# The attention heads' output turned by DMA instead of TensorE: rows of features in memory, sums beside them, division and split on GpSimd and VectorE

## Chip, cores and metric

One core of one Trainium2 chip. The metric is the device time of one execution in microseconds (us), median of several runs.

## What is computed

`x` is 2 sequences of 1024 tokens with 512 features, all in float32. Six sublayers follow one another, each on the layer norm of `x` and each added to `x`:

```python
x = x + 0.5 * _L0_ffn_ref(_layernorm(x))    # one 512x512 product, columns scaled
x = x + _L0_attn_ref(_layernorm(x))         # 32 heads of 16, 8 key heads, rotary, causal, then @ w_o.T + b_o
x = x + 0.5 * _L0_ffn_ref(_layernorm(x))
x = x + 0.5 * _L1_ffn_ref(_layernorm(x))    # 512x512 product and 8 rank-16 experts, top 2
x = x + _L1_attn_ref(_layernorm(x))         # 8 heads of 32, causal, then @ w_o.T + b_o
x = x + 0.5 * _L1_ffn_ref(_layernorm(x))
```

The part that the change touches is the end of both attentions: `out = softmax(scores) @ v`, and `out @ w_o.T + b_o`.

## The kernel before

The five engines run their own programs, tied by semaphores. The two sequences (`b`) go one after the other; a sequence is three chains of 128-token tiles with an attention behind each of the first two: FFN_A and the products of QKV0, the first attention (`A0`), WO0, FFN_B, MOE_A and the products of QKV1, the second attention (`A1`), WO1 and MOE_B. Every product is three passes: an operand is split into a high part, rounded for TensorE's fast float32 form, and the low rest (hi x hi, hi x lo, lo x hi).

**An attention** works in units: 8 units of 4 heads in `A0`, 4 units of 2 heads in `A1`. A unit has two halves `c` of 512 queries; half 0 has 4 steps, half 1 has 8, one for each block of 128 keys (`steps`, 12 per unit). For a step TensorE makes the scores (L983, L977), ScalarE the exponentials into `probs` (L1431), GpSimd the causal mask of the diagonal blocks (L1542), and TensorE, two or three steps later, the value products into the PSUM bank `heads` (L999). There the heads stand as rows: the features of each head and beside them, through a column of ones in `v_mem`, the sum of its exponentials. When a half is done, ScalarE copies `heads` to `heads_raw` (L1418).

**The ring.** Softmax needs each row's maximum ahead of its exponentials. About one unit ahead TensorE makes the scores a second time for that, into three PSUM banks in turn (`ring`, L871), and VectorE reduces each bank (`maxes`, L1204 for masked ones, L1208 for the rest). Twice per unit VectorE makes the shifts (L1247 to L1253), TensorE turns them (L876), VectorE copies them out (`shiftT`, L1217), and SyncE stores them as operand rows of the scores. A third kind of item stands in the ring: `norm`, one per half of a unit. TensorE turns `heads_raw` with four transposes (L881), VectorE takes the reciprocals of the sums (L1227) and multiplies (L1232) into `features`, tokens in rows. `plan_ring` fixes the order of all items, and where among the steps they stand; item i is written only when item i-3 has been read (`ring_free`), and TensorE runs its list in order:

```python
kind, u, n = a.ring[i - 3]
read, m = {"max": (s["max_done"], u * a.unit_max_ops + a.max_ops_to[n]), "shift": (s["shiftT"], 2 * u + n + 1),
           "norm": (s["normed"], 2 * u + n + 1)}[kind]
pe.wait_ge(read.sem, read.at(b, m))
```

**The product of WO** (WO0, WO1): for each tile `turn_x` transposes `features` (L765, four transposes in WO0 and two in WO1), ScalarE copies the high part (L1315), VectorE subtracts the low part (L1055), TensorE makes 12 (WO0) or 6 (WO1) matmuls (L779 to L781), and VectorE adds the result to `x` (L1071), to which GpSimd has added the bias (L1484). `prod` has two banks, so tile t waits for the addition of tile t-2. In a chain the engines go by ticks: tick i holds the transposes of tile i, the product of tile i-1 and, on VectorE, the addition of tile i-2.

**SyncE** issues every DMA, in one order: in the first attention the rows of the shifts, and for unit u+3 the queries, once unit u's scores are done; the weights of FFN_B and MOE_A in units 3 and 4.

The names that the change and the prediction use: `plan_ring` (L191 on), `load_shifts` (L598), `rotated_attention` (L648), `standard_attention` (L687), `turn_x` (L751), `begin` (L768), `ring_item` (L856), `ring_read` (L1187), and `attention` of each engine.

## Time and profile before

| | |
|---|---|
| median of 3 runs | 1358.18 us (1355.22 to 1362.18) |
| the profiled execution | 1344.81 us, of which the span from the first to the last instruction 1343.1 us |
| TensorE busy (matmuls, weight loads) | 1205.7 us (90%), 753.2 us (56%) |
| VectorE busy | 953.5 us (71%) |
| ScalarE busy | 671.2 us (50%) |
| GpSimd busy | 375.2 us (28%) |
| mean granted TensorE clock | 0.928 |
| bytes moved by DMA | 76.20 MB |

Engines in the rows: PE is TensorE's matmuls, PEld its weight loads, DVE VectorE, ACT ScalarE, POOL GpSimd, SP SyncE. The matmuls overlap one another in the rows, so the distance from start to start tells what one costs. Time 0 is the first instruction. The first attention of the first sequence lies at 116 to 358 us, the second at 531 to 619 us.

### The profile page before, as it was taken

The page shows a single profiled execution, that of the slowest core. Times are in us where ns is not written, and L with a number is a line of the kernel's source. Part 1 is how long each engine was busy: PE and PEld are TensorE (multiplying, and loading weights), DVE is VectorE, ACT ScalarE, POOL GpSimd, SP SyncE. Part 2 cuts the span into 40 slices and gives each one's busy share as a digit, 9 for nine tenths or more (in the row PEclk, how much of TensorE's full clock was granted, in tenths as well). Part 3 has the DMA queues.
Part 4 walks back from the last instruction along what each step waited for, and adds up shares of the span by engine and source line. Part 5 has one row for each costly group of instructions (what it writes and reads, how often), then busy time and mean ns, then how long its engine had stood idle before and what let it go on. Part 6 is the DMA issues. An engine that isn't in the chain of part 4 may idle for free.

```text
span 1343.1 us, 21792 instructions
## 1 busy us (share of the span) xinstructions
PE 1205.7 (90%) x6800; PEld 753.2 (56%) x6800; DVE 953.5 (71%) x2990; ACT 671.2 (50%) x1023; POOL 375.2 (28%) x505
## 2 busy tenths in 40 slices
PE   4998999999899877998879999999988988879988
PEld 1875444443388865444868744444435887744368
DVE  5889889898166676653659798999962667576365
ACT  2621666666655452544436036666665554435542
POOL 0431411122254400114614323122213542002162
PEclk9996899999999997999979858999999999869999
DMA  8374411220010020100140742112200100120001
GB/s 317 120 196 87 125 29 26 57 65 3 1 49 1 1 47 19 55 2 0 63 175 23 189 130 70 26 26 57 66 2 0 50 1 17 32 72 2 1 8 56
DMA packets 37285, 76.20 MB, mean 57 GB/s; under 512 B 5084, under 2 KB 6620, under 8 KB 37036
## 3 DMA queue, kind: packets, MB, share of 16 engines
q1 hardware_dynamic: 37176, 74.82, 19.2%
q8 instruction: 60, 0.98, 0.3%
q14 instruction: 49, 0.40, 0.1%
HBM read 48.98 MB, written 27.08 MB: 57 GB/s over the span
## 4 chain that ended last, share of the span: by engine, by line
PE 64%; DVE 19%; issue 5%; POOL 5%; ACT 5%; DMA 1%; DVEq 0%; SPq 0%; ACTq 0%; POOLq 0%
PE bank L999 16%; PE bank L871 12%; PE bank L779 5%; PE bank L780 5%; PE bank L781 5%; DVE maxes L1208 5%; PE bank L983 4%; PE bank L977 3%; DVE unused L1204 3%; PE bank L765 3%; DVE ops L1152 3%; PE bank L881 2%; POOL x L1484 2%; POOL w_odd L1466 2%; ACT ops L1356 2%
## 5 line engine op out<-in xcount | busy, mean ns | idle before, releaser
L1431 ACT ACTIVATE probs<-bank 128x1024 f32<-128x1024 f32 (+3 forms) x416 | 367.9, 911 | 320.4 <-PE bank L983 220.3
L871 PE MATMUL bank<-ops 48*128 48x512 f32 (+3 forms) x960 | 321.8, 436 | 34.5 <-DVE maxes L1204 17.2
L1204 DVE CUSTOM_DVE_ANT_0 unused<-bank,causal 128x128 bf16<-128x128 f32 (+3 forms) x640 | 279.5, 486 | 47.7 <-PE bank L871 44.1
L1542 POOL TENSOR_SCALAR_AFFINE_SELECT probs<-probs 128x256 f32<-128x256 f32 (+1 forms) x256 | 118.8, 464 | 640.3 <-ACT probs L1431 640.0
L871 PEld LDWEIGHTS bank<-ops 48*128 48x128 f32 (+1 forms) x960 | 163.0, 206 | 218.9 <-DVE maxes L1204 96.0
L999 PE MATMUL bank<-probs,v_mem 128*17 128x512 f32 (+6 forms) x1920 | 252.2, 517 | 6.1 <-ACT heads_raw L1418 5.6
L1208 DVE TENSOR_REDUCE maxes<-bank 128x1 f32<-128x512 f32 x320 | 207.4, 684 | 40.7 <-PE bank L871 39.2
L983 PE MATMUL bank<-ops 50*128 50x512 f32 (+2 forms) x640 | 175.9, 448 | 5.0 <-ACT probs L1431 4.8
L779 PE MATMUL bank<-ops,xT 128*128 128x512 f32 (+1 forms) x288 | 116.2, 403 | 19.6 <-DVE x L1068 11.6
L983 PEld LDWEIGHTS bank<-ops 50*128 50x128 f32 x640 | 86.6, 197 | 57.9 <-ACT probs L1431 29.5
L1473 POOL TENSOR_TENSOR rstd<-var_eps,minus_half 128x1 f32<-128x1 f32 x96 | 52.7, 549 | 215.1 <-DVE var_eps L1046 214.5
L1315 ACT CAST xT<-bank 128x512 fp32r<-128x512 f32 (+1 forms) x96 | 52.6, 548 | 118.0 <-PE bank L765 117.9
L1055 DVE TENSOR_TENSOR xT<-bank,xT 128x512 fp32r<-128x512 f32 (+1 forms) x96 | 61.5, 643 | 67.5 <-ACT xT L1315 67.1
L780 PE MATMUL bank<-ops,xT 128*128 128x512 f32 (+1 forms) x288 | 105.5, 366 | 0.0
L781 PE MATMUL bank<-ops,xT 128*128 128x512 f32 (+1 forms) x288 | 105.5, 366 | 0.0
L999 PEld LDWEIGHTS bank<-probs,v_mem 128*17 128x17 f32 (+1 forms) x1920 | 40.9, 99 | 77.1 <-issue 52.0
L1374 ACT ACTIVATE probs<-x,ln_bias,rstd 128x512 f32<-128x512 f32 x96 | 78.3, 816 | 3.2
L779 PE MATMUL bank<-w_odd,xT 128*128 128x324 f32 (+1 forms) x192 | 72.8, 379 | 5.8 <-DVE x L1068 2.7
L1227 DVE RECIPROCAL inv_sum<-bank 128x16 f32<-128x16 f32 (+1 forms) x48 | 11.3, 234 | 92.6 <-PE bank L881 92.6
L779 PEld LDWEIGHTS bank<-ops,xT 128*128 128x128 f32 x288 | 56.4, 196 | 31.2 <-issue 21.4
L765 PE MATMUL bank<-identf,probs 128*128 128x128 f32 x384 | 57.8, 280 | 16.0 <-ACT probs L1374 16.0
L1042 DVE BATCH_NORM_STATS2 stats<-x 128x6 f32<-128x512 f32 x96 | 65.8, 686 | 3.7 <-DMA x<-x_dram 3.3
(117 smaller groups left out, 1965.5 us busy)
## 6 DMA issues: line engine op xcount, KB each, us to landing
query_rows_dram<-ops SPq DMA_DIRECT2D x48, 256.0 KB, 3.8
ops<-query_rows_dram SPq DMA_DIRECT2D x64, 192.0 KB, 4.4
w_odd<-staging_wqkv SPq DMA_DIRECT2D x4, 1536.0 KB, 7.3
x<-x_dram SPq DMA_DIRECT2D x16, 256.0 KB, 6.1
ops<-ops SPq DMA_DIRECT2D x16, 256.0 KB, 3.0
out_dram<-x SPq DMA_DIRECT2D x16, 256.0 KB, 2.0
staging_wqkv<-wqkv_dram SPq DMA_DIRECT2D x2, 1536.0 KB, 15.8
key_rows_dram<-ops SPq DMA_DIRECT2D x24, 128.0 KB
```

The source lines that it names most:

```text
L765: last = nc.tensor.transpose(turn[n % 2][:, k * P:(k + 1) * P], src[:, k * P:(k + 1) * P], identf[:])
L779: mm(dst, x_hi[:, k, :], hi[:, k, :], start=(k == 0), stop=False)
L780: mm(dst, x_hi[:, k, :], lo[:, k, :], start=False, stop=False)
L781: last = mm(dst, x_lo[:, k, :], hi[:, k, :], start=False, stop=(k == kc - 1 and not lora))
L871: last = mm(dst[:, h * w:(h + 1) * w], queries(a, u)[rows, t // 4, hi, t % 4 * P:(t % 4 + 1) * P], keys(a, u, hi)[rows, HALF * kp:HALF * k ...
L983: last = mm(dst, keys(a, u, 0)[rows, block], queries(a, u)[rows, c, heads_of[0]:heads_of[-1] + 1, columns], start=True, stop=True)
L999: last = mm(heads[a.head_rows * h:a.head_rows * h + a.dim + 1, q0 - HALF * c:HALF], v[:, j, a.kv_head(u, r, i), :], probs[:, e % 6, n, fir ...
L1204: V.tensor_tensor_reduce(unused[:, masked % 3, 0:w], part, causal[:, HALF - w:], 1.0, NEG, ALU.add, ALU.max, dst).then_inc(s["max_done"].s ...
L1208: V.tensor_reduce(dst, part, AX.X, ALU.max).then_inc(s["max_done"].sem, 1)
L1374: A.activation(xn[n % XN_SLOTS], x[:, t, :], ACT.Identity, bias=ln_bias[:, i, :], scale=rstd[:, i, :]).then_inc(xn_ready.sem, 1)
L1431: A.activation(probs[:, e % 6, :, 0:cols], scores[:, 2 * (e % 2):2 * (e % 2) + 2, 0:cols], ACT.Exp, scale=a.scale).then_inc(s["exp"].sem, 1)
L1542: G.affine_select(out=p, in_=p, compare_op=ALU.is_ge, fill=0.0, base=0, pattern=pattern, channel_multiplier=-1).then_inc(s["masked"].sem, 1)
```

## The change

The `norm` items leave the ring, and WO's tiles are no longer transposed. Instead:

- SyncE stores each half's `heads_raw` (128x512, 256 KB) to memory and, when that has landed, loads it back as rows of features, 64 partitions for a unit: the features to `head_in`, each head's sum, repeated over the rows of its features, to `head_sum` (`load_heads`). Two units fill the 128 partitions. All this stands in SyncE's one order, between the loads of the shifts and of the queries.
- Once two units (`k`) are staged, VectorE takes the reciprocal of the whole `head_sum` half, 128x512 (`inverse_sums`). GpSimd multiplies, copies the high part and subtracts the low part into `heads_T`, in memory of `ops` that is free by then (`heads_out`, three operations of 128x512). This is done during units 2, 4, 6 (`A0`) and unit 2 (`A1`): the reciprocals behind steps 2 and 6 on VectorE, the three operations ahead of steps 4 and 7 on GpSimd.
- The last two units' halves are done on VectorE alone (`last_heads`: reciprocal, multiply, copy, subtract): half 0 at the end of the attention, half 1 in tick 3 of the next chain, ahead of the addition of tile 1.
- WO's products read `heads_T` as they are. ScalarE may copy a new half once the old one is stored.
- `xT` moves into `ops`; MOE_A's weights, whose memory `heads_T` takes, are loaded after WO0 and split at FFN_B's tiles 4 to 7 instead of 2 to 5.

Counts for the program: 192 + 96 transposes go; 48 stores of 256 KB, 96 loads of 128 KB, 24 reciprocals of 128x512, 16 times three operations on GpSimd and 8 times three on VectorE come.

```diff
-                if slot == 0:
-                    for c in range(2):
-                        e = s - self.lag - 2 - self.last_step[c]
-                        if e >= 0 and e % ns == 0 and e // ns < self.units:
-                            dst.append(("norm", e // ns, c))
...
-TURNS = [it for ticks in TICKS for k in ticks for it in k.turns]
+TURNS = [it for ticks in TICKS for k in ticks for it in k.turns if it[0] not in WO_ATT]
...
-        xT = sb("xT", [P, 2, 2, KC, P], F32R)
-        ops = sb("ops", [P, 20, SEQ], F32R)
+        ops = sb("ops", [P, 22, SEQ], F32R)
...
+        xT = ops_flat[:, 20480:22528].rearrange("p (m n k c) -> p m n k c", m=2, n=2, k=KC)
+        head_in, head_sum = (features[:, 2 * HALF * n:2 * HALF * (n + 1)].rearrange("p (c s) -> p c s", c=2) for n in range(2))
+        head_out = features[:, 4 * HALF:6 * HALF].rearrange("p (c s) -> p c s", c=2)
...
+        def heads_T(a, part, k):
+
+            first = ((4096, 5120, 6144, 7168), (8192, 9216, 21504, 14336)) if a is A0 else ((1024, 3072), (4096, 5120))
+            return ops_flat[:, first[part][k]:first[part][k] + SEQ]
...
+            def load_heads(b, st, u, c):
+
+
+                a, s = ATT[st], qs[st]
+                lanes = slice(64 * (u % 2), 64 * (u % 2) + 64)
+                sp.wait_ge(s["raw"].sem, s["raw"].at(b, 2 * u + c + 1))
+                wait(sp, s["staged"][c], b, 32 * u)
+                sp.dma_start(raw_rows[c], heads_raw[:, c, :]).then_inc(s["dumped"][c].sem, 16)
+                sp.wait_ge(s["dumped"][c].sem, s["dumped"][c].at(b, 16 * (u + 1)))
+                if u == 0 and c == 0 and a.rope:
+                    sp.wait_ge(s["lo"].sem, s["lo"].at(b, 6))
+                if u > 1:
+                    sp.wait_ge(s["out"].sem, s["out"].at(b, 3 * (2 * (u // 2 - 1) + c) + 1))
+                rows = raw_rows[c].rearrange("(h r) s -> h r s", r=a.head_rows)
+                sp.dma_start(head_in[lanes, c, :], rows[:, 0:a.dim, :]).then_inc(s["staged"][c].sem, 16)
+                sp.dma_start(head_sum[lanes, c, :], rows[:, a.dim:a.dim + 1, :].to_broadcast([a.unit_heads, a.dim, HALF])
+                             ).then_inc(s["staged"][c].sem, 16)
...
+                    load_heads(b, QKV0, u, 0)
...
-                    if u in (3, 4):
-                        load_weights(b, FFN_B if u == 3 else MOE_A)
+                    if u == 3:
+                        load_weights(b, FFN_B)
+                    load_heads(b, QKV0, u, 1)
...
-                for u in range(1, A1.units):
-                    load_shifts(b, QKV1, u, 0)
-                    load_shifts(b, QKV1, u, 1)
+                for u in range(A1.units):
+                    if u + 1 < A1.units:
+                        load_shifts(b, QKV1, u + 1, 0)
+                    load_heads(b, QKV1, u, 0)
+                    if u + 1 < A1.units:
+                        load_shifts(b, QKV1, u + 1, 1)
+                    load_heads(b, QKV1, u, 1)
...
+                load_weights(b, MOE_A)
...
-                pe.wait_ge(xT_ready.sem, xT_ready.at(b, TURN_NO[st, t] + 1))
+                if st in WO_ATT:
+                    a, s = WO_ATT[st], qs[QKV0 if st == WO0 else QKV1]
+                    pe.wait_ge(s["out"].sem, s["out"].at(b, 3 * (a.units - 2)))
+                    pe.wait_ge(s["last"].sem, s["last"].at(b, 3 * (t // 4 + 1)))
+                else:
...
+                    x_in = ([heads_T(WO_ATT[st], part, k)[:, t * P:(t + 1) * P] for k in range(chunks_of[st])] for part in range(2))
...
-                    c = 2 * u + n
-                    pe.wait_ge(s["raw"].sem, s["raw"].at(b, c + 1))
-                    for j in range(4):
-                        last = nc.tensor.transpose(dst[:, j * P:(j + 1) * P],
-                                                   heads_raw[:, c % 2, j * P:(j + 1) * P], identf[:])
...
+                    if c > 0 and i == 3:
+                        last_heads(b, QKV0 if c == 1 else QKV1, 1)
...
-                    V.reciprocal(inv_sum[:, 0:4 * nh].unsqueeze(2), blocks[:, :, d:d + 1]).then_inc(s["inv"].sem, 1)
...
-                    V.tensor_tensor(dst, src.rearrange("p (t h r) -> p t h r", t=4, h=nh)[:, :, :, 0:d],
-                                    inv_sum[:, 0:4 * nh].rearrange("p (t h) -> p t h", t=4).unsqueeze(3)
-                                    .to_broadcast([P, 4, nh, d]), ALU.mult).then_inc(s["normed"].sem, 1)
+
+            def inverse_sums(b, st, k, c):
+
+                a, s = ATT[st], qs[st]
+                dve.wait_ge(s["staged"][c].sem, s["staged"][c].at(b, 32 * (2 * k + 2)))
+                V.reciprocal(head_sum[:, c, :], head_sum[:, c, :]).then_inc(s["inverse"].sem, 1)
+
+            def last_heads(b, st, c):
+
+                a, s = ATT[st], qs[st]
+                k = a.units // 2 - 1
+                inverse_sums(b, st, k, c)
+                hi, lo = (heads_T(a, part, k)[:, HALF * c:HALF * (c + 1)] for part in range(2))
+                dve.wait_ge(s["inverse"].sem, s["inverse"].at(b, 2 * k + c + 1))
+                dve.wait_ge(s["out"].sem, s["out"].at(b, 3 * (2 * (k - 1) + c + 1)))
+                V.tensor_tensor(head_out[:, c, :], head_in[:, c, :], head_sum[:, c, :], ALU.mult).then_inc(s["last"].sem, 1)
+                dve.wait_ge(s["last"].sem, s["last"].at(b, 3 * c + 1))
+                V.tensor_copy(hi, head_out[:, c, :]).then_inc(s["last"].sem, 1)
+                dve.wait_ge(s["last"].sem, s["last"].at(b, 3 * c + 2))
+                V.tensor_tensor(lo, head_out[:, c, :], hi.bitcast(F32), ALU.subtract).then_inc(s["last"].sem, 1)
 
             def attention(b, st):
-                for i in range(max(ATT[st].begun.values()), ATT[st].ring_len):
-                    ring_read(b, st, i)
+                a = ATT[st]
+                ring_no = max(a.begun.values())
+                for g, step in [(-1, [a.ring_first])] + list(enumerate(a.ring_at)):
+                    upto = len(a.ring_first) + sum(len(slot) for before in a.ring_at[:g + 1] for slot in before)
+                    for i in range(ring_no, upto):
+                        ring_read(b, st, i)
+                    ring_no = upto
+                    u, k_ = divmod(g, len(a.steps))
+                    if u % 2 == 0 and 0 < u < a.units and k_ in (2, 6):
+                        inverse_sums(b, st, u // 2 - 1, k_ // 6)
+                last_heads(b, st, 0)
 
             def shift_parts(b, st, u, c):
...
-                                act.wait_ge(s["ring_full"].sem, s["ring_full"].at(b, a.norm_at[ch - 2] + 1))
+                                act.wait_ge(s["dumped"][c].sem, s["dumped"][c].at(b, 16 * (ch // 2)))
...
-                        if nb < BATCH and nst not in WO_ATT and 2 <= t < 2 + chunks_of[nst]:
-                            split_chunk(nb, nst, t - 2)
+                        first = 4 if nst == MOE_A else 2
+                        if nb < BATCH and nst not in WO_ATT and first <= t < first + chunks_of[nst]:
+                            split_chunk(nb, nst, t - first)
...
+            def heads_out(b, st, k, c):
+
+                a, s = ATT[st], qs[st]
+                n = 3 * (2 * k + c)
+                hi, lo = (heads_T(a, part, k)[:, HALF * c:HALF * (c + 1)] for part in range(2))
+                pool.wait_ge(s["inverse"].sem, s["inverse"].at(b, 2 * k + c + 1))
+                G.tensor_tensor(head_out[:, c, :], head_in[:, c, :], head_sum[:, c, :], ALU.mult).then_inc(s["out"].sem, 1)
+                pool.wait_ge(s["out"].sem, s["out"].at(b, n + 1))
+                G.tensor_copy(hi, head_out[:, c, :]).then_inc(s["out"].sem, 1)
+                pool.wait_ge(s["out"].sem, s["out"].at(b, n + 2))
+                G.tensor_tensor(lo, head_out[:, c, :], hi.bitcast(F32), ALU.subtract).then_inc(s["out"].sem, 1)
+
...
+                    if u % 2 == 0 and u > 0 and k_ in (4, 7):
+                        heads_out(b, st, u // 2 - 1, k_ // 7)
```

**Where the instructions move.** VectorE's list in unit 2 of the first attention (maxima of unit 3), before: behind the unit's first shifts stands one reduction, then the small reciprocal and the multiply of a `norm` item.

```order
L1251 TENSOR_SCALAR shifts<-maxes 128x16
L1253 SCALAR_TENSOR_TENSOR shifts<-maxes,shifts 128x16
L1208 TENSOR_REDUCE maxes<-bank 128x1
L1227 RECIPROCAL inv_sum<-bank 128x16
L1232 TENSOR_TENSOR features<-bank,inv_sum 128x4x64
L1208 TENSOR_REDUCE maxes<-bank 128x1 x2
L1217 COPY shiftT<-bank 32x128
L1208 TENSOR_REDUCE maxes<-bank 128x1
```

The same place now: the reciprocal of 128x512 (L1247 of the changed kernel) stands behind the shifts and ahead of the reductions, and the `norm` item's two are gone.

```order
L1287 TENSOR_SCALAR shifts<-maxes 128x16
L1289 SCALAR_TENSOR_TENSOR shifts<-maxes,shifts 128x16
L1247 RECIPROCAL features<-features 128x512
L1232 TENSOR_REDUCE maxes<-bank 128x1 x3
L1241 COPY shiftT<-bank 32x128
L1232 TENSOR_REDUCE maxes<-bank 128x1
L1228 ISA unused,maxes<-bank,causal 128x128
```

Four banks later (step 6), now: the second reciprocal stands among the reductions of one tile of queries.

```order
L1228 ISA unused,maxes<-bank,causal 128x256
L1228 ISA maxes 128x1
L1232 TENSOR_REDUCE maxes<-bank 128x1 x3
L1247 RECIPROCAL features<-features 128x512
L1232 TENSOR_REDUCE maxes<-bank 128x1
L1228 ISA unused,maxes<-bank,causal 128x384
```

It splits a run of four reductions that had the `norm` item's two instructions behind it. VectorE's list at the end of the first attention, now, from the last copy of shifts:

```order
L1241 COPY shiftT<-bank 32x128
L1247 RECIPROCAL features<-features 128x512
L1257 TENSOR_TENSOR features<-features 128x512
L1259 CAST ops<-features 128x512
L1261 TENSOR_TENSOR ops<-features,ops 128x512
L1093 TENSOR_TENSOR x<-bank,x 128x512
L1247 RECIPROCAL features<-features 128x512
L1257 TENSOR_TENSOR features<-features 128x512
L1259 CAST ops<-features 128x512
L1261 TENSOR_TENSOR ops<-features,ops 128x512
L1093 TENSOR_TENSOR x<-bank,x 128x512 x3
```

The second half's four instructions stand between the additions of tiles 0 and 1; before, `norm` items and WO's subtractions (L1055) stood here. SyncE's list from the first unit on, before:

```order
L606 DMA ops<-shiftT 1x8x128 x8
L639 DMA ops<-query_rows_dram 48x2x512 x4
L606 DMA ops<-shiftT 1x8x128 x8
L639 DMA ops<-query_rows_dram 48x2x512 x4
L606 DMA ops<-shiftT 1x8x128 x8
```

and now, with a store and two loads per half between the shift rows and the queries:

```order
L605 DMA ops<-shiftT 1x8x128 x4
L615 DMA raw_rows_dram<-heads_raw 128x512
L622 DMA features<-raw_rows_dram 64x1x512
L623 DMA features<-raw_rows_dram 64x1x512
L605 DMA ops<-shiftT 1x8x128 x4
L656 DMA ops<-query_rows_dram 48x2x512 x4
L615 DMA raw_rows_dram<-heads_raw 128x512
L622 DMA features<-raw_rows_dram 64x1x512
L623 DMA features<-raw_rows_dram 64x1x512
L605 DMA ops<-shiftT 1x8x128 x4
```

The shift rows of a unit, four transfers per half, were neighbours and are now parted by a half's store and loads.

## Rows read from the trace of the kernel before

**Rows 1.** The page, part 1: busy us, share of the span, instructions.

```profile
PE 1205.7 (90%) x6800; PEld 753.2 (56%) x6800; DVE 953.5 (71%) x2990; ACT 671.2 (50%) x1023; POOL 375.2 (28%) x505
```

**Rows 2.** Windows: length, busy us (instructions) by engine, granted clock, DMA share, GB/s.

```profile
188.70:216.90 28.20, 27.45 (x198) 11.67 (x194) 26.23 (x92) 18.99 (x22) 5.77 (x12) 1.00 0.14 30
334.80:358.00 23.20, 19.49 (x164) 6.36 (x160) 1.37 (x4) 18.41 (x23) 7.11 (x14) 1.00 0.01 2
575.50:599.00 23.50, 21.60 (x108) 10.36 (x106) 14.65 (x48) 10.65 (x14) 3.25 (x8) 1.00 0.01 3
```

**Rows 3.** Groups by line: busy us, mean ns of one, idle before and releasers.

```profile
L881 PE MATMUL bank<-identf,heads_raw 128*128 128x128 f32 x192 | 31.5, 288 | 5.5 <-ACT heads_raw L1418 3.1 <-DVE maxes L1208 2.3
...
L1227 DVE RECIPROCAL inv_sum<-bank 128x16 f32<-128x16 f32 (+1 forms) x48 | 11.3, 234 | 92.6 <-PE bank L881 92.6
...
L1269 DVE RECIPROCAL probs<-probs 128x512 f32<-128x512 f32 x1 | 3.4, 3354 | 1.2 <-ACT probs L1305 1.2
```

**Rows 4.** Timeline, unit 2 of the first attention: start, us, engine, operation, [idle before].

```profile
193.28 0.59 ACT L1418 COPY heads_raw<-bank 128x512 f32<-128x512 f32 x1
...
195.90 0.17 DVE L1253 SCALAR_TENSOR_TENSOR shifts<-maxes,shifts 128x16 fp32r<-128x16 f32 x1
...
197.85 0.28 PE L876 MATMUL bank<-identf,shifts 128*32 128x128 f32 x1
...
204.78 2.60 DVE L1208 TENSOR_REDUCE maxes<-bank 128x1 f32<-128x512 f32 x4
...
206.24 0.66 PE L881 MATMUL bank<-identf,heads_raw 128*128 128x128 f32 x4 [0.22 <-DVE maxes L1208]
...
206.82 0.49 PE L983 MATMUL bank<-ops 50*128 50x512 f32 x2
...
208.78 0.18 PEld L871 LDWEIGHTS bank<-ops 48*128 48x128 f32 x1 [0.85 <-DVE features L1232]
```

**Rows 5.** DMA transfers: count, KB each, median us to landing; last, all of `query_rows_dram`.

```profile
query_rows_dram<-ops SPq DMA_DIRECT2D x48, 256.0 KB, 3.8
...
out_dram<-x SPq DMA_DIRECT2D x16, 256.0 KB, 2.0
...
ops<-staging_base SPq DMA_DIRECT2D x2, 1296.0 KB, 8.1
...
DMA to landing us min/median/max: 2.8/4.0/6.8
```

**Rows 6.** Timeline, ends of the attentions and starts of WO0 and WO1.

```profile
346.12 0.62 ACT L1418 COPY heads_raw<-bank 128x512 f32<-128x512 f32 x1
...
357.86 0.58 ACT L1418 COPY heads_raw<-bank 128x512 f32<-128x512 f32 x1 [1.24 <-PE bank L999]
...
366.54 0.60 PE L765 MATMUL bank<-identf,features 128*128 128x128 f32 x4
...
369.74 0.60 PE L765 MATMUL bank<-identf,features 128*128 128x128 f32 x4
...
373.27 0.49 PE L779 MATMUL bank<-w_odd,xT 128*128 128x512 f32 x1
...
618.51 0.58 ACT L1418 COPY heads_raw<-bank 128x512 f32<-128x512 f32 x1 [1.91 <-PE bank L999]
...
632.11 0.69 DVE L1071 TENSOR_TENSOR x<-bank,x 128x512 f32<-128x512 f32 x1 [0.93 <-POOL x L1484]
```

**Rows 7.** Timeline: the same VectorE operation beside a mask and alone; GpSimd's additions.

```profile
187.59 0.64 POOL L1542 TENSOR_SCALAR_AFFINE_SELECT probs<-probs 128x512 f32<-128x512 f32 x1 [1.86 <-ACT probs L1431]
187.60 0.65 DVE L1247 TENSOR_TENSOR maxes<-maxes 128x16 f32<-128x16 f32 x1
...
551.91 0.17 DVE L1247 TENSOR_TENSOR maxes<-maxes 128x8 f32<-128x8 f32 x1
...
357.29 2.49 POOL L1484 TENSOR_TENSOR x<-x,bo 128x512 f32<-128x512 f32 x2
```

**Rows 8.** A window of one unit, as rows 2; a stop of TensorE in the timeline.

```profile
221.50:252.20 30.70, 30.13 (x196) 12.48 (x198) 26.53 (x92) 19.04 (x24) 5.80 (x12) 0.89 0.13 28
...
332.52 0.27 PE L876 MATMUL bank<-identf,shifts 128*32 128x128 f32 x1 [2.36 <-DVE shifts L1253]
```

89 lines of the change are left out of this document (39 added, 50 removed).

## Prediction

> **What bounds the kernel now.** I read the busy shares first, then a table of windows by stage, then the timeline inside one unit of attention. Over the whole span TensorE is 90% busy and VectorE 71% [rows 1], which reads as a TensorE kernel with room on VectorE. The windows say otherwise. In one unit of the first attention (28.2 us) TensorE is busy 27.5 us and VectorE 26.2 us, 93% [rows 2]: both are near their limit, coupled through the three PSUM banks of `ring`. In the last unit, whose maxima are all done, VectorE has 1.4 us of work in 23.2 us; in the second attention 14.7 us in 23.5 us [rows 2]. The timeline shows the coupling: at 208.78 the load of a maximum bank waited 0.85 us for VectorE [rows 4]. So a question decides: does work added to VectorE sit where TensorE has three banks of lead, or stop it?
>
> **Removed from TensorE.** The 48 `norm` items of the ring: 192 transposes [rows 3], and on VectorE 48 small reciprocals and multiplies. One item holds TensorE from 206.24 to the next matmul at 206.82, 0.6 us [rows 4]. Between 0.44 us (what four transposes cost in WO's tiles, below) and 0.85 us (the wait that the multiply imposes on the bank behind it) [rows 4]; I take 0.6. Per sequence 13 of the 16 items of the first attention stand in units 0 to 6, where TensorE is full: 26 x 0.6 = -15.6 us. Two stand in the last unit, where ScalarE is busy 18.4 of 23.2 us and TensorE 19.5: priced at nothing, at most -2.4 us in all. In the second attention 7 of 8: 14 x 0.6 = -8.4 us. The last item of each attention belongs to the start of WO, below.
>
> **Added to VectorE.** 24 reciprocals of 128x512. The one such reciprocal of the trace took 3.35 us [rows 3]. Sixteen stand inside the attentions: 6 per sequence in the first (units 2, 4, 6), 2 in the second. The order shows the places. Behind the shifts of a unit: VectorE is free at 196.07, the reciprocal would end at 199.4, the first of the three banks behind it is read at 200.1. TensorE fills three banks, then comes to the shift's transposition, which stood at 197.85 and, with a norm item gone, at 197.25: it stops 2.8 us [rows 4]. Behind step 6: the reductions of 0.65 us begin at 204.78, three of them end at 206.7, the reciprocal at 210.1, the fourth reduction at 210.7; the bank that waits for it was loaded at 208.78, now 208.2: 2.5 us [rows 4]. VectorE's own sum gives a floor: a unit with two reciprocals and without two norms needs 26.2 - 1.3 + 6.7 = 31.6 us, against 27.0 us for TensorE, so 2.3 us each at least; the top is 3.35. I take 2.7: 12 x 2.7 = +32.4 us. In the second attention VectorE has a third of its time free, between 0 and 3.35 us each; the same reading, with banks at half the pace, gives 1.4: 4 x 1.4 = +5.6 us.
>
> **The round trip.** ScalarE's copy of the heads is now stored to memory (256 KB) and read back twice (128 KB each). Nearest rows: a store of 256 KB lands in 2.0 us (the output) or 3.8 us (the queries); transfers of the queries, loads and stores together, land in 2.8 us at best, 4.0 in the median and 6.8 at worst [rows 5]. Store and loads one after the other are thus 4.8 us (2.0 + 2.8) to 10.6 us (3.8 + 6.8). I take 6.5, nearer the short end, since these transfers come alone and the query rows come in bursts of four to six; 8.5 is the upper end that I give a chance. The Trainium skill (DMA: Bandwidth & Descriptors, Anatomy of one DMA) puts a transfer at some 2 us plus its bytes at 436 GB/s; as an estimate that makes the trip 4.9 us and the whole sum 6 us lower than mine. Inside the attentions the trip is covered: the second half's copy ends at 193.9 and its sums are needed at 206.7 [rows 4]. In the second attention, whose units last 23.5 us instead of 28.2, the cover is near its end: priced at nothing, up to 1 us each. SyncE's waits for the heads stand ahead of the next unit's shift rows and query loads; the shift rows are only ready at the end of a unit, the queries are a unit early: nothing. If that cover is gone, the scores of the next unit are late.
>
> **GpSimd.** Three operations of 128x512 per half, about 1.3 us each by its additions of the same size (two in 2.49 us) [rows 7]: 4 us in steps 4 to 7, where it has no mask: nothing. Late, it would hold the masks of step 8 and with them TensorE's value products.
>
> **The start of WO.** Before, in the first layer, ScalarE's last copy ended at 358.4 and tile 3's product began at 373.27 [rows 6]. Now tile 0 needs only the first half, copied at 346.7, so the products begin at about 358.5. Tile 3, however, waits for the sum of tile 1, and that stands on VectorE behind the second half's reciprocal, multiply, copy and subtraction: 358.4 + 6.5 + (3.35 + 0.7 + 0.4 + 0.7 + 0.2) + 0.7 = 371.0, that is 2.3 us earlier. Then each of the tiles left saves its four transposes: a tile lasts 3.20 us (366.54 to 369.74), twelve products at 0.23 are 2.76, so 0.44 each, 2.0 us. Together -4.3 us, twice: -8.6 us. In the second layer the copy ends at 619.1 and the same chain gives 631.7, tile 3's sum by 633.5; it began at 632.11 [rows 6]. With six products per tile there is less to hide it: +1.4 us, and 0.6 for a cold clock: +2, twice: +4 us. The ends are -6 and -1 us, and 0 and +4 us.
>
> **Port.** VectorE's multiply and subtraction read two SBUF operands while GpSimd adds WO's bias. The row shows what that does: the maximum of two SBUF tiles took 0.65 us where a mask of GpSimd began 0.01 us earlier, 0.17 us where none ran [rows 7]. Eight last halves, two such operations each, at most 1.3 us: 0 to +10 us on the path; I take +3. The Trainium skill (SBUF — State Buffer, Who interferes with whom) has the same rule: such an instruction and a GpSimd instruction that reads SBUF exclude each other. By that rule, the trace agrees (0.65 against 0.17 us).
>
> **Clock.** A stretch of a unit at granted clock 0.89 took 30.7 us, one at 1.00 28.2 us [rows 2, 8]: a fall costs 2.5 us. TensorE now stands still 16 times for over 1 us. It once stood 2.36 us (before 332.52) and kept clock 1.00 [rows 8]. 0 to +12 us; I take one more fall: +3.
>
> **MOE_A's weights** are loaded after WO instead of in unit 4, and split two tiles later: the load (8.1 us [rows 5]) ends before tile 4, four tiles of 3.2 us on. Nothing; if late, ScalarE waits for it. The copies on ScalarE and subtractions on VectorE of WO's transposes go too, behind TensorE's work.
>
> **Sum.** -15.6 - 8.4 + 32.4 + 5.6 - 8.6 + 4 + 3 + 3 = +15.4 us on the profiled execution's 1344.8 us: 1360 us. The median of the runs shown is 1358.2, 13 us above it; on that scale, which I predict, 1373.6 us.
>
> **Rivals.** *The banks hide the reciprocals* (faster). VectorE's idle 29% of the span speaks for it, the 93% of a unit against. With 0.5 us per reciprocal the sum is 15.4 - 38 + 8 = -15 us, 1343.5 us. It turns at 1.4 us per reciprocal. Chance 0.11. *It cancels*: floor of 2.3 us, norm items worth 0.85 us, second attention hidden: 27.6 - 22 - 11.9 + 0 - 8.6 + 4 + 3 + 3 = -5, and up to +6 us: 1353 to 1364 us. Chance 0.21. *The trip is late*: at 13 us instead of 6.5, each start of WO loses 6 us and four halves of the second attention wait for it: +28 us on mine, 1402 us. The queue is busy with little else, and rows 5 have the like of it landing in 2 to 4 us. Chance 0.06. *The clock falls at every other stop*: 8 x 2.5 - 3 = +17 us, 1391 us. Chance 0.10. *Forecast*: 0.52.
>
> Everything at its cheap end gives -18 us, at its dear end +64 us; both at once are unlikely. 1351 to 1390 us holds the forecast, the cancelling case and most of the clock's. Within 0.5% (6.8 us, about what a measurement of this kernel can tell from no change): 0.21; faster 0.11; slower 0.68.
>
> **What would show it.** In the profile after: 24 reciprocals of 3.35 us; behind each of the 12 in the first attention a wait of TensorE for VectorE of 2 to 3 us; units 2, 4, 6 at about 32.4 us and units 1, 3, 5 at 27.0 us; 288 transposes gone; a store that lands in 2 to 4 us; tile 3 of WO near 13 us behind the last copy. I am wrong if even units last under 30 us, or if VectorE waits for the staged heads inside an attention.

## The result, and the profile after

| | before | after |
|---|---|---|
| median of the runs, us | 1360.18 (4 runs, 1355.22 to 1364.52) | 1425.90 (4 runs, 1407.22 to 1431.48) |
| profiled execution, us (its span) | 1344.81 (1343.1) | 1427.49 (1425.7) |
| mean granted clock of TensorE | 0.928 | 0.864 |
| ratio of the times | | 1.0487 (95%: 1.0417 to 1.0557) |

The change made the kernel 4.9% slower. The sign was forecast; the size, +15 us, was not: it is +66 us by the medians and +82.6 us between the two profiled spans. Medians are over all runs of a kernel, while ratios leave out those in which the same kernel ran in a slower state of the chip; the traces of the run with one-column reciprocals and of the last run below are of that state.

The first part of the page of the kernel after (busy us, share, instructions), to be held against [rows 1]:

```profile
PE 1234.2 (87%) x6512; PEld 750.8 (53%) x6512; DVE 1007.0 (71%) x2910; ACT 658.1 (46%) x991; POOL 427.6 (30%) x553
```

TensorE has 288 instructions fewer and is busy 28.5 us longer. That can only be if the same instructions run slower. The granted clock has two levels in the records, full (1.00) and half; a mean of 0.928 over 1343.1 us is 193 us at half clock, 0.864 over 1425.7 us is 388 us.

Windows of the first attention after the change: units 2, 3, 4, 6 and the last (columns as [rows 2]: length; busy us of PE, PEld, DVE, ACT, POOL; clock; DMA share; GB/s):

```profile
188.10:227.00 38.90, 33.51 (x190) 13.66 (x186) 32.48 (x97) 19.23 (x23) 12.06 (x18) 0.74 0.18 49
227.00:254.10 27.10, 26.37 (x192) 10.89 (x188) 24.46 (x82) 18.90 (x22) 5.80 (x13) 1.00 0.26 70
254.10:289.70 35.60, 31.39 (x192) 13.61 (x188) 31.56 (x90) 19.18 (x22) 12.08 (x19) 0.76 0.29 83
317.90:358.00 40.10, 33.38 (x187) 13.76 (x183) 32.01 (x91) 19.20 (x22) 12.62 (x19) 0.71 0.09 28
358.00:381.90 23.90, 22.07 (x132) 6.05 (x128) 2.54 (x1) 17.72 (x21) 4.58 (x11) 0.70 0.13 45
```

Odd units last 27.1 us, as forecast (27.0; unit 5 of this sequence, at clock 0.94, 28.2). Even units were to last 32.4 and last 35.6 to 40.1, in the second sequence 38.2 to 42.0. Take unit 2 beside unit 3: TensorE stands still 5.4 us against 0.7, so the stops cost 4.7 us; and it is busy 33.5 us against 26.4 with the same work, so the clock costs 7.1 us. The whole kernel's term for the clock was 3 us.

The same over both first attentions, before and then after (windows, columns as above):

```profile
116.20:355.60 239.40, 227.23 (x1489) 96.16 (x1489) 197.44 (x667) 153.98 (x180) 54.65 (x100) 0.91 0.20 51
779.40:1018.30 238.90, 226.72 (x1489) 96.25 (x1489) 197.56 (x667) 153.98 (x180) 54.66 (x100) 0.92 0.20 51
116.90:381.90 265.00, 242.73 (x1429) 100.42 (x1429) 210.49 (x644) 154.46 (x180) 73.42 (x118) 0.78 0.25 71
816.90:1085.10 268.20, 246.95 (x1427) 101.42 (x1428) 210.18 (x644) 154.66 (x180) 73.40 (x118) 0.77 0.25 70
```

TensorE stands still 19 us more than before and is busy 36 us longer, although the transposes of the `norm` items are gone.

The groups of the reciprocal and of the maxima's matmuls (busy, mean ns; idle before and what ended it); last, the latter's group before the change, with 436 ns instead of 469 and 34.5 us idle instead of 53.4:

```profile
L1247 DVE RECIPROCAL features<-features 128x512 f32<-128x512 f32 x24 | 80.3, 3347 | 105.2 <-DMA features<-raw_rows_dram 105.2
...
L899 PE MATMUL bank<-ops 48*128 48x512 f32 (+3 forms) x960 | 343.1, 469 | 53.4 <-DVE maxes L1232 31.0
...
L871 PE MATMUL bank<-ops 48*128 48x512 f32 (+3 forms) x960 | 321.8, 436 | 34.5 <-DVE maxes L1204 17.2
```

The first stop of unit 2 in the timeline (start, us, engine, operation, [idle before]):

```profile
195.48 3.35 DVE L1247 RECIPROCAL features<-features 128x512 f32<-128x512 f32 x1
198.75 1.82 DVE L1232 TENSOR_REDUCE maxes<-bank 128x1 f32<-128x512 f32 x3
...
199.43 0.40 PE L904 MATMUL bank<-identf,shifts 128*32 128x128 f32 x1 [2.61 <-DVE maxes L1232]
...
200.35 0.62 PE L899 MATMUL bank<-ops 48*128 48x512 f32 x1
...
208.89 0.50 PE L899 MATMUL bank<-ops 48*128 48x512 f32 x2
```

TensorE stops 2.61 us (forecast 2.8) at the place that was named. What the forecast lacked is in the next lines: the matmul of 48x512 takes 0.62 us behind the stop and 0.50 us from 208.89 on.

Where the 82.6 us went, by the starts of the first and the last score matmul of each attention:

| stretch, us (sequence 0 / 1) | before | after | difference |
|---|---|---|---|
| up to the first attention | 116.2 | 116.9 | +0.7 |
| first attention | 239.4 / 238.9 | 265.0 / 268.2 | +54.9 |
| WO0 up to the second attention | 175.2 / 171.8 | 172.6 / 172.7 | -1.7 |
| second attention | 85.1 / 84.9 | 88.5 / 90.2 | +8.7 |
| WO1 and the rest | 163.5 / 68.1 | 173.9 / 77.6 | +19.9 |

### The profile page after: what moved, and what is told of

Read it like the earlier page. It is cut to its first block, busy times and chain, and to the rows that moved or that the text cites. A ratio compares the mean times of both kernels' runs of the same rounds, so it can differ in the third digit from the quotient of the medians.

```text
span 1425.7 us, 21287 instructions
## 1 busy us (share of the span) xinstructions
PE 1234.2 (87%) x6512; PEld 750.8 (53%) x6512; DVE 1007.0 (71%) x2910; ACT 658.1 (46%) x991; POOL 427.6 (30%) x553
## 3 DMA queue, kind: packets, MB, share of 16 engines
q1 hardware_dynamic: 50552, 99.99, 23.1%
## 4 chain that ended last, share of the span: by engine, by line
PE 59%; DVE 20%; issue 9%; ACT 4%; DMA 4%; POOL 4%; SPq 1%; DVEq 0%; ACTq 0%; POOLq 0%
PE bank L1020 16%; PE bank L899 12%; PE bank L1004 5%; PE bank L802 5%; PE bank L804 5%; PE bank L803 5%; DVE maxes L1232 4%; DVE unused L1228 3%; PE bank L998 3%; DVE ops L1174 2%; PE bank L785 2%; ACT ops L1393 2%; DMA features<-raw_rows_dram 2%; DVE features L1247 2%; POOL x L1522 1%
## 5 line engine op out<-in xcount | busy, mean ns | idle before, releaser
L899 PE MATMUL bank<-ops 48*128 48x512 f32 (+3 forms) x960 | 343.1, 469 | 53.4 <-DVE maxes L1232 31.0
L1020 PE MATMUL bank<-probs,v_mem 128*17 128x512 f32 (+6 forms) x1920 | 284.5, 585 | 6.2 <-ACT heads_raw L1456 5.0
L1004 PE MATMUL bank<-ops 50*128 50x512 f32 (+2 forms) x640 | 204.2, 511 | 1.4 <-ACT probs L1469 1.2
L1247 DVE RECIPROCAL features<-features 128x512 f32<-128x512 f32 x24 | 80.3, 3347 | 105.2 <-DMA features<-raw_rows_dram 105.2
L802 PE MATMUL bank<-ops 128*128 128x512 f32 (+1 forms) x288 | 117.5, 408 | 41.7 <-issue 22.5
L803 PE MATMUL bank<-ops 128*128 128x512 f32 (+1 forms) x288 | 107.2, 372 | 0.0
L804 PE MATMUL bank<-ops 128*128 128x512 f32 (+1 forms) x288 | 107.2, 372 | 0.0
L1352 ACT CAST ops<-bank 128x512 fp32r<-128x512 f32 x96 | 55.2, 584 | 99.3 <-PE bank L785 99.0
L1077 DVE TENSOR_TENSOR ops<-bank,ops 128x512 fp32r<-128x512 f32 x96 | 65.0, 686 | 36.1 <-ACT ops L1352 35.8
L802 PEld LDWEIGHTS bank<-ops 128*128 128x128 f32 x288 | 57.8, 201 | 53.5 <-issue 44.9
L802 PE MATMUL bank<-w_odd,ops 128*128 128x324 f32 (+1 forms) x192 | 73.9, 385 | 11.7 <-issue 4.6
L1404 ACT ACTIVATE ln_bias<-minus_mean,rstd 128x1 f32<-128x1 f32 x96 | 28.2, 294 | 119.1 <-POOL rstd L1511 118.6
```

Of the source, the lines that this page charges most:

```text
L802: mm(dst, x_hi[k], hi[:, k, :], start=(k == 0), stop=False)
L803: mm(dst, x_hi[k], lo[:, k, :], start=False, stop=False)
L804: last = mm(dst, x_lo[k], hi[:, k, :], start=False, stop=(k == kc - 1 and not lora))
L899: last = mm(dst[:, h * w:(h + 1) * w], queries(a, u)[rows, t // 4, hi, t % 4 * P:(t % 4 + 1) * P], keys(a, u, hi)[rows, HALF * kp:HALF * k ...
L1004: last = mm(dst, keys(a, u, 0)[rows, block], queries(a, u)[rows, c, heads_of[0]:heads_of[-1] + 1, columns], start=True, stop=True)
L1020: last = mm(heads[a.head_rows * h:a.head_rows * h + a.dim + 1, q0 - HALF * c:HALF], v[:, j, a.kv_head(u, r, i), :], probs[:, e % 6, n, fir ...
```

## The experiments

Times are medians; ratios are to runs of the kernel before on the same chip, whose medians were 1349.9 to 1353.6 us. Kernels are compared by their ratios.

### The reciprocals alone

```diff
+                    if u % 2 == 0 and 0 < u < a.units and k_ in (2, 6):
+                        V.reciprocal(dummy[:, :], dummy[:, :]).then_inc(dummy_sem, 1)
```

> The kernel before, with nothing of the change but its 8 reciprocals of 128x512 per sequence in the attentions' loops (in place on a tile of ones, at the same places in VectorE's order: after steps 2 and 6 of units 2, 4, 6 of the first attention and of unit 2 of the second). Theory A (a stop of 2.5 to 3 us behind each of them lowers TensorE's clock for the steps that follow, and this is most of the loss): even units of the first attention go from 28 to about 39 us, and the whole is 80 us (60 to 95) above the kernel before, with the share of half-clock time about doubled. Rival B (only the stops count, 12 x 2.7 + 4 x 1.4 us, and the rest of the loss comes from the DMA path and from GpSimd): +38 us (30 to 45), and the half-clock time stays near that of before.

Measured: 1433.8 us, ratio 1.0617 (1.0541 to 1.0693), +81 us by the medians: theory A's number, twice what the stops alone would give. Unit 2 here (window, columns as above):

```profile
190.00:229.00 39.00, 34.33 (x198) 14.90 (x194) 32.74 (x94) 19.21 (x22) 5.82 (x12) 0.74 0.10 22
```

Against the 28.2 us of [rows 2] it stands still 3.9 us more and is busy 6.9 us more at clock 0.74. Nothing of the round trip is in this kernel, so neither DMAs nor GpSimd are needed for the loss in the even units. The half-clock time of the span went from 193 us to 347 us (clock 0.878), not quite to the double that was expected.

### The reciprocals taken out

```diff
-                V.reciprocal(head_sum[:, c, :], head_sum[:, c, :]).then_inc(s["inverse"].sem, 1)
+                w = HALF if k == a.units // 2 - 1 else 1
+                V.reciprocal(head_sum[:, c, 0:w], head_sum[:, c, 0:w]).then_inc(s["inverse"].sem, 1)
```

> The changed kernel, with the reciprocals in the loops cut from 512 columns to 1, so that all heads but the last pair of each attention are multiplied by their sums and not by the inverses. Everything else (the round trips, GpSimd's operations, the last reciprocals, the waits) stays. Theory A: the even units fall to the odd ones' 27 us, and the kernel gains 86 us: 1340 us (1325 to 1355), below the kernel before. Rival B (stops only): 1388 us (1380 to 1396), above the kernel before.

Measured: 1350.9 us, ratio 0.9969 (0.9926 to 1.0012). Against the changed kernel's 1.0487 the in-loop reciprocals are worth 5.2% of some 1352 us, 70 us. The time is in theory A's range, and the price far from B's +38; with the first run (+83 us by the ratio) it is much the same price from both sides. By the ratios it is 16 us short of A's 86, and the trace tells why: one thing besides long reciprocals makes VectorE late. A one-column reciprocal at step 6 of unit 4, and TensorE (timeline):

```profile
261.57 0.17 DVE L1248 RECIPROCAL features<-features 128x1 f32<-128x1 f32 x1 [3.00 <-DMA features<-raw_rows_dram]
...
262.37 0.68 PE L899 MATMUL bank<-ops 48*128 48x384 f32 x1 [2.33 <-DVE maxes L1232]
```

VectorE waited 3.0 us in its order for the second half's loads, and TensorE stood 2.3 us behind it: a wait there stops it as a reciprocal does. The unit took 31.3 us. The forecast had said that this trip was covered. The loads were issued at 256.31; the store ahead of them, issued at 248.00, had taken 8.3 us behind four loads of query rows and the 1024 KB of FFN_B's weights in the same queue.

One unit of this trace doesn't fit a price by stops: unit 2 of the second sequence (window) took 33.3 us at clock 0.74, though TensorE stood still only 0.3 us in it. A fall of the clock can come without a stop.

```profile
854.00:887.30 33.30, 32.96 (x190) 13.20 (x186) 25.80 (x96) 18.92 (x22) 12.10 (x18) 0.74 0.22 57
```

### The same work in pieces

```diff
-                    if u % 2 == 0 and 0 < u < a.units and k_ in (2, 6):
-                        inverse_sums(b, st, u // 2 - 1, k_ // 6)
+                    if u % 2 == 0 and 0 < u < a.units and k_ in (0, 1, 2, 3, 8, 9, 10, 11):
+                        c, j = divmod((0, 1, 2, 3, 8, 9, 10, 11).index(k_), 4)
+                        inverse_sums(b, st, u // 2 - 1, c, j)
```

> The changed kernel, with each reciprocal in the loops in 4 pieces of 128 columns (about 0.87 us each), in steps 0, 1, 2, 3 for the first half and 8, 9, 10, 11 for the second, and GpSimd's operations after them (steps 5 and 13). VectorE does the same work; replayed on the ring, the stops sum to 14.1 us in a sequence's first attention (17.6 now), but the longest is 1.2 us and not 3. Theory A (the length of a stop decides, by the clock): no falls, 1365 us (1350 to 1385). Rival C (VectorE's total work in the even units decides, however it is cut): 1415 us (1405 to 1425).

Measured: 1416.2 us, ratio 1.0503 (1.0414 to 1.0592): rival C's number, no gain on the changed kernel's 1.0487. Theory A in the form "one long stop does it" fell here. Units 2 and 3 (windows):

```profile
186.60:219.70 33.10, 30.24 (x191) 12.92 (x188) 29.47 (x91) 19.07 (x22) 8.93 (x16) 0.85 0.19 57
219.70:256.30 36.60, 34.37 (x192) 14.71 (x188) 28.04 (x93) 19.21 (x22) 8.80 (x16) 0.67 0.20 52
```

Unit 2 gained, and unit 3, which had been 27.1 us, lost it again at clock 0.67. At its start two pieces and the maxima of the unit's first steps meet, and the ring falls behind little by little (timeline):

```profile
220.92 0.95 DVE L1249 RECIPROCAL features<-features 128x128 f32<-128x128 f32 x1
221.06 0.28 PE L904 MATMUL bank<-identf,shifts 128*32 128x128 f32 x1 [0.66 <-DVE maxes L1228]
...
222.15 0.95 DVE L1249 RECIPROCAL features<-features 128x128 f32<-128x128 f32 x1
222.29 0.58 PE L899 MATMUL bank<-ops 48*128 48x256 f32 x1 [0.94 <-DVE maxes L1228]
```

Stops of 0.7 and 0.9 us one after the other, and the matmuls behind them run at half clock (48x256 in 0.58 us; 0.28 us at 220.00, ahead of the stops). So the revised theory, called A' from here on: in a full unit VectorE has 2.6 us to spare (24.5 of 27.1), and what goes beyond becomes idle time of TensorE wherever it stands; idle time of one or a few microseconds in this stretch, in one piece or in several, is mostly followed by many microseconds at half clock. It is a tendency, with exceptions both ways (a unit of the one-column run fell without a stop, and the stop of 2.36 us of [rows 8] had no fall behind it). Piece length is no lever.

### Half the work, and another place

```diff
-                        V.reciprocal(dummy[:, :], dummy[:, :]).then_inc(dummy_sem, 1)
+                        V.reciprocal(dummy[:, 0:HALF // 2], dummy[:, 0:HALF // 2]).then_inc(dummy_sem, 1)
```

> The kernel before with its 8 reciprocals per sequence as in the first run of this study, at 256 columns instead of 512 (1.68 us each instead of 3.35). Proportional (VectorE's work is what is paid, at any length): half of the +81 us, +40 (33 to 47). Threshold (the ring's banks hide some 0.65 us of each, and stops of 1 us don't lower TensorE's clock): 16 x 1.0 = +16 us (8 to 22), half-clock time in the first attentions as before (40 us each).

Measured: 1380.1 us, ratio 1.0282 (1.0146 to 1.0418), +26.5 us by the medians and +38 us by the ratio. The median lies between the two theories, the ratio at the first, and its interval is wide: the times don't decide. The trace does, against the threshold. Unit 2 (window):

```profile
189.30:222.60 33.30, 31.71 (x198) 13.52 (x194) 29.39 (x94) 19.07 (x23) 5.82 (x12) 0.85 0.12 26
```

It is 5.1 us longer than in [rows 2], and its clock is 0.85: shorter stops brought falls too. The first attentions have some 65 and 73 us at half clock, against 41 and 40 before, where the threshold wanted no more than before. The first attentions took 253.4 and 257.8 us, +33 us in all, about half of the first run's effect there (281.0 and 268.8: +71 us).

```diff
-                    if u % 2 == 0 and 0 < u < a.units and k_ in (2, 6):
+                    if u % 2 == 0 and 0 < u < a.units and k_ in (3, 11):
```

> The kernel before with the 8 reciprocals of 512 columns per sequence as in the first run, after steps 3 and 11 instead of 2 and 6, where the ring's order has few maxima. Replayed on the ring the stops are 13.7 instead of 17.6 us in a first attention. If the place decides: +60 us or less. If VectorE's total decides (26.3 of a unit's 28.3 us are busy before, so 6.7 more can't fit wherever they stand): +81 us again (70 to 90).

Measured: 1418.0 us, ratio 1.0542 (1.0445 to 1.0640), +64 us by the medians, +73 by the ratio. The median lies between the two, the ratio in the second's range. The place is worth 10 us by the ratios, whose intervals overlap, and 17 of 81 us by the medians; the unit after each even one, 28.3 to 30.6 us before, now lasts 33.8 or 35.9 us. VectorE's total is most of what is paid.

### The loads head by head

```diff
-                sp.dma_start(head_in[lanes, c, :], rows[:, 0:a.dim, :]).then_inc(s["staged"][c].sem, 16)
+                for h in range(a.unit_heads):
+                    to = slice(lanes.start + a.dim * h, lanes.start + a.dim * (h + 1))
+                    sp.dma_start(head_in[to, c, :], rows[h, 0:a.dim, :]).then_inc(s["staged"][c].sem, 16)
```

(and the sums in the same way, ahead of them)

> The changed kernel, with the loads of heads and sums issued head by head (4 + 4 of 16 rows per half in the first attention, 2 + 2 of 32 rows in the second), the sums first. The trace shows the loads at 109 and at 51 GB/s and the store at 400. Theory D (a load whose outermost dimension counts 4 or 2 goes by so many of the 16 engines, which makes the round trip 7.4 and 12.3 us and WO1's start 10 us late): both loads go at over 150 GB/s, the trips take about 6 and 7 us, the wait ahead of WO1's first reciprocal falls by 5 us or more, and the whole by 13 us (8 to 22). Rival E (the round trip is bound by its two landings of 2 us and the wait on the engine's order): no change within 4 us.

Why this was asked: the DMA view of the changed kernel around a store and its two loads in the second attention (40 slices of 636 to 650 us; share of the engines in tenths, then GB/s):

```profile
DMA  1111149511111110000020011111111495111100
GB/s 53 53 53 47 53 170 415 223 53 47 59 47 47 59 41 0 0 0 0 6 18 12 12 47 47 59 47 53 53 47 53 193 410 211 47 53 53 47 29 6
```

The 256 KB store runs at 415 GB/s, the loads at 53, and in the first attention at 109 (slices of 371 to 380 us):

```profile
GB/s 0 0 0 0 0 0 0 0 291 382 410 82 0 73 0 0 0 0 0 46 18 18 9 46 82 109 109 91 91 109 109 109 100 82 36 0 0 0 0 0
```

Two heads outermost in the one, four in the other: the rate goes as that number, some 27 GB/s each. The Trainium skill has this rule (DMA: Bandwidth & Descriptors, Why a DMA increments its semaphore by 16 and not by 1): a DMA runs on k engines, where k is the largest number up to 16 that divides the slowest dimension of size above 1 on both sides. By that rule k is 2 and 4 here, and 16 for a head's 16 or 32 rows; the traces agree for 2 and 4 (53 and 109 GB/s), the forecast did not use it.

Measured: 1392.5 us, ratio 1.0295 (1.0226 to 1.0365): 1.9 points below the changed kernel, 26 us, more than theory D's 8 to 22 and far from E. In the same kind of window (642 to 648 us) the loads now run at 82 to 191 GB/s, where over 150 was expected, and from the first half's store (issued at 631.64) to its reciprocal (636.91) pass 5.3 us instead of 12.3; SyncE pays for it with more issues per half, one every 0.46 us or so: 8 in the first attention and 4 in the second, instead of 2. The last half's chain in the second layer, ScalarE's copy to tile 3's addition, was 23.1 us (below) and is 15.7. WO1's stretches fell from 173.9 and 77.6 us to 162.3 and 72.6, the second attentions by 3.6 and 4.2, where VectorE had waited 1.5 and 1.8 us for a second half's loads.

### Taking the inverse elsewhere

```diff
+                G.tensor_tensor(head_sum[:, c, :], head_sum[:, c, :], minus_one[:, 0:1].to_broadcast([P, HALF]), ALU.pow
+                                ).then_inc(s["inverse"].sem, 1)
```

> The changed kernel, with the loops' reciprocals taken from VectorE and given to GpSimd, as a power with exponent -1 over 128x512 ahead of its multiplication. GpSimd's power of 128x1 takes 0.55 us in the trace and its multiplication of 128x512 1.27 us. Optimist: a power of 128x512 takes under 4 us, GpSimd has room for it (12 of an even unit's 39 us busy), and the whole comes to about 1345 us. Pessimist: the 0.45 us above GpSimd's shortest instructions is paid for every few columns; a power of 128x512 then takes tens of us, the masks behind it come late, and the whole is above 1600 us.

Measured: 2602.8 us. The group (busy, mean ns of one):

```profile
L1569 POOL TENSOR_TENSOR features<-features,minus_one 128x512 f32<-128x512 f32 x16 | 1310.8, 81927 | 0.0
```

82 us for one power of 128x512, 0.16 us a column. GpSimd is no place for it.

The other way is to do as the kernel before did and invert each sum once, not once per feature. The run below sends the sums of all units but the last from `raw_rows` to a tile of 128x16, inverts them there, stores them and loads them broadcast:

```diff
+                    sp.dma_start(sums[:, c, 0:HALF // n], rows[:, a.dim, :].rearrange("h (x f) -> h x f", x=n))
...
+                V.reciprocal(sums[:, c, 0:n], sums[:, c, 0:n]).then_inc(s["inverted"].sem, 1)
...
+                sp.dma_start(inv_rows[c, 0:a.unit_heads, :].rearrange("h (x f) -> (h x) f", x=n), sums[:, c, 0:HALF // n])
...
+                sp.dma_start(head_sum[lanes, c, :], inv_rows[c, 0:a.unit_heads, :].unsqueeze(1)
+                             .to_broadcast([a.unit_heads, a.dim, HALF])).then_inc(s["staged"][c].sem, 16)
```

> The changed kernel, with the sums of every unit but the last sent to a tile of 128x16 (128x8 in the second attention), inverted there by VectorE (16 columns, some 0.2 us by the row of the kernel before), stored and sent as inverses to the heads' lanes; the last unit's heads and sums are loaded head by head as in the run on the loads. Everything is computed. If theories A and D hold together: the even units take the odd ones' 27 to 28 us and WO1's start gains as in the run of the loads: 1320 us (1305 to 1340), below the kernel before. Rival F (the two more DMAs in SyncE's queue per half unit and their longer trip hold back the shift rows, so that the gain is a new wait): 1350 us or more.

Measured: 1427.3 us, ratio 1.0565 (1.0378 to 1.0753): wrong by 107 us, though VectorE's busy time is 40 us less than in the changed kernel. Neither theory: TensorE did not wait for shift rows, but for VectorE, and VectorE for a DMA (waits: engine, what; us, times, longest). Four of the 20, of 10.4 to 11.8 us, stand in the last units, where no maxima are left and they hold up little; the other 16, 44 us in all, stand in the full ones:

```profile
DVE sums L1284 <- DMA sums<-raw_rows_dram: 89.2, 20, 11.8
```

SyncE's part of it (timeline): the store of the second half issued at 169.84 lets the load of its sums go only at 175.48, since the query rows' four loads (1.82 us of issues ahead of it) are in the same queue; VectorE was told to invert at step 5.

```profile
169.84 0.43 SPq L619 DMA_DIRECT2D raw_rows_dram<-heads_raw  x1
175.48 0.55 SPq L628 DMA_DIRECT2D sums<-raw_rows_dram  x1
```

This is the one-column run's finding at a larger size, and it supports A': a VectorE that waits stops TensorE like one that works. It also says that a cheaper instruction is no gain if it comes with a wait in the same order.

The next run inverts the second half's sums three steps later and multiplies it in the odd unit. Beside the lines shown it loads the features head by head and stores the inverses behind the next half's heads; what each of these edits gave was not tried alone.

```diff
-                    if k_ == 5 and 0 < u < a.units:
+                    if k_ == 8 and 0 < u < a.units:
                         invert(b, st, u - 1, 1)
...
-                    if u % 2 == 0 and u > 0 and k_ in (4, 9):
-                        heads_out(b, st, u // 2 - 1, k_ // 9)
+                    if g >= 2 * ns and g % (2 * ns) in (4, 13):
+                        heads_out(b, st, u // 2 - 1, 0 if k_ == 4 else 1)
```

> The run with compact inverses, in whose trace VectorE stood 89 us in 20 waits for the sums (the second half's store lands behind the query rows' loads, some 5 us after its issue, so its sums aren't there at step 5), again with the second half's inversion after step 8 instead of 5, its multiplication a step into the next unit, the inverses' store behind the first half's heads in SyncE's queue, and the features loaded head by head. Theory G (each of VectorE's waits for a DMA in the loop stops TensorE as a long reciprocal does, and with them gone the loops run at 27 us a unit): first attentions of 236 us (256 and 264 before this edit), the second 84 (95), the whole 1335 us (1322 to 1350), below the kernel before. Rival F (SyncE's queue with two more DMAs per half unit holds back the shift rows): 1360 or more, with TensorE waiting at steps 4 or 0 for shift rows.

Measured: 1351.9 us, ratio 0.9984 (0.9944 to 1.0024): the whole loss of the change is gone, 75 us to the last run. It is 17 us above theory G's number, and one unit holds the difference in each sequence; units 4 and 5 of the first (windows), and the place (timeline):

```profile
243.20:270.30 27.10, 26.30 (x188) 10.81 (x186) 25.25 (x90) 18.87 (x22) 8.88 (x16) 1.00 0.36 106
270.30:310.60 40.30, 37.17 (x188) 15.21 (x187) 27.33 (x96) 19.26 (x22) 8.83 (x16) 0.62 0.22 54
```

```profile
277.51 1.26 POOL L1612 TENSOR_TENSOR features<-features 128x512 f32<-128x512 f32 x1 [4.11 <-DMA features<-inv_rows_dram]
...
281.62 1.48 PE L1056 MATMUL bank<-probs,v_mem 128*17 128x384 f32 x8 [2.96 <-POOL probs L1640]
```

GpSimd stood 4.1 us for the inverses with masks of the unit's first steps behind it, TensorE 3.0 us for a mask, and the unit ran at clock 0.62: 2.3 us more idle than unit 4, but 10.9 us more busy.

```diff
-                    if g >= 2 * ns and g % (2 * ns) in (4, 13):
-                        heads_out(b, st, u // 2 - 1, 0 if k_ == 4 else 1)
+                    if g >= 2 * ns and g % (2 * ns) in (4, 16):
+                        heads_out(b, st, u // 2 - 1, g % (2 * ns) // 16)
```

> The last run but one (compact inverses, inverted later) with one edit: GpSimd's three operations on the second half stand at step 4 of the odd unit and not at step 1. In its trace unit 5 took 40 us and the others 27.2, since the inverses landed 4.1 us after GpSimd stood waiting for them at step 1, with the masks of steps 1 to 3 behind the wait; TensorE then stopped 3.3 us and went on at half clock. Steps 4 to 7 have no masks. If that wait is the whole of it: unit 5 takes 27 us in both sequences and unit 7 is 2 us shorter: 1352 - 2 x 12 - 2 x 2 = 1324 us (1315 to 1338), 2% below the kernel before. Rival: the wait moves to SyncE's queue (the second half's load of unit 4 waits for this multiplication, and the shift rows of unit 6 stand behind it), and unit 5 or 6 stays above 30 us: 1345 us or more.

Measured: 1338.0 us over 12 runs, ratio 0.9886 (0.9846 to 0.9927): 1.1% faster than the kernel before, and the best version found. Units 2 and 3 (windows):

```profile
186.60:213.80 27.20, 26.41 (x190) 10.89 (x186) 25.33 (x90) 18.88 (x23) 8.97 (x15) 1.00 0.26 72
213.80:241.00 27.20, 26.37 (x190) 10.89 (x186) 25.34 (x90) 18.87 (x23) 8.93 (x15) 1.00 0.27 71
```

In the profiled execution units 1 to 5 last 27.2 us, with one exception: unit 5 of the second sequence, 33.5 us, 13.7 of it at half clock. The same kind of wait stands at its start (timeline): VectorE waited 1.4 us for the sums of a half whose store was issued at 917.96, and TensorE 1.6 us for VectorE.

```profile
922.21 0.25 DVE L1290 RECIPROCAL sums<-sums 128x16 f32<-128x16 f32 x1 [1.44 <-DMA sums<-raw_rows_dram]
...
922.90 0.58 PE L935 MATMUL bank<-ops 48*128 48x256 f32 x1 [1.62 <-DVE maxes L1264]
```

The first attentions take 231.4 and 238.2 us; they took 239.4 and 238.9 before. The gain is short of the 2% expected, and the end of the program still pays 3.5 us more than before (71.6 against 68.1).

### Both cuts together

```diff
+                w = HALF if k == a.units // 2 - 1 else 1
...
-                    if u % 2 == 0 and 0 < u < a.units and k_ in (2, 6):
+                    if u % 2 == 0 and 0 < u < a.units and k_ in (2, 8):
...
-                    if u % 2 == 0 and u > 0 and k_ in (4, 7):
+                    if u % 2 == 0 and u > 0 and k_ in (4, 9):
```

(on the kernel with the loads head by head)

> The changed kernel with both cuts together: the loops' reciprocals on 1 column (all heads but the last pair of each attention are multiplied by their sums), the loads head by head, and the second half's place after step 8 instead of 6, where its loads have landed. This is the changed kernel without VectorE's long instructions and without its waits for DMAs in the loops. If the two costs add and nothing else is behind: 1426 - 75 - 33 - some 10 for the waits that the one-column run still had at steps 6 and 7 = 1310 us (1298 to 1325). If the head-by-head loads only helped by relieving the loops that the reciprocals had slowed: 1340 us, near the one-column run's 1351.

Measured: 1360.5 us, ratio 0.9949 (0.9897 to 1.0001). Expected by the sum was a ratio near 0.97, by the other case 0.99; it is the other case, but its reason isn't shown by it. The trace has a stop of its own: step 11 of the even units lasts 2.49 instead of 1.29 us in three of the four units 2 and 4, where the masks of steps 9 to 11 now stand behind GpSimd's 3.1 us of operations, and behind two of these three the next unit has 13.7 and 20.5 us at half clock. So this run met a wait of its own making, and what the two cuts give without one stays open; the run above, which leaves nothing out, was no slower (ratio 0.9886).

## Why the prediction was right or wrong, point by point

- **The norm items.** Forecast 0.6 us each. Odd units went from 28.3 to 27.1 us with two items gone: 0.6 each. Right.
- **The stops behind the reciprocals.** Forecast 5.4 us per even unit. Units 2, 4 and 6 stand still 4.7, 3.5 and 6.0 us more than unit 3. Place and cause were right, the size slightly too large; the rival *the banks hide the reciprocals* is out.
- **The clock.** This step failed: "I take one more fall: +3", with +12 as the end of its range. In units 2, 4 and 6 TensorE is busy 7.1, 5.0 and 7.0 us longer than in unit 3, 19 us in this sequence, and the last units behind them, at clock 0.70 here, take 23.8 and 24.0 us against 20.8 before. Two readings led there: a fall was priced at 2.5 us from one unit at clock 0.89 [rows 8], though units here go down to 0.71, and one stop of 2.36 us that kept clock 1.00 [rows 8] was taken as the rule. In [rows 8] TensorE was busy 30.1 of the 30.7 us, so that fall had no stop ahead of it and said nothing of what follows one. The rival *the clock falls at every other stop* had the right mechanism and 1391 us; with the 6.4 us that a unit lost here in place of 2.5 its sum would have been some 1420 us. That this is near the 1425.9 measured is in part luck, since the rival leaves out the late loads below.
- **The second attention.** Forecast -2.8 us (5.6 for the stops, -8.4 for the norm items); measured +8.7. Units 2 last 28.8 and 30.7 us against 23.4. "Priced at nothing, up to 1 us each" was said of the trip; the loads of two heads at 53 GB/s make it 12.3 us there (copied by 637.1, reciprocal at 649.45; its store was issued at 637.14 and its loads only at 641.72, behind the loads of the half before). The head-by-head loads gave 7.8 us of it back.
- **The round trip.** Taken as 6.5 us. In the first attention it is 7.4 us (copied by 372.0, reciprocal at 379.37; by 385.1, at 392.42): near. In the second, at 12.3 us, it is the late trip of the rival that had 0.06. The estimate of 4.9 us from the Trainium skill (DMA: Bandwidth & Descriptors, Anatomy of one DMA) was further off; the page gives those figures for DMAs that GpSimd issues, and these are SyncE's. The rows that the 6.5 us were read from were queries and outputs; none had a small number outermost. That VectorE would not wait inside an attention was wrong too: two of its 8 waits for the loads are inside the second attentions (1.5 and 1.8 us), and four in the one-column run, where the reciprocals no longer delayed VectorE (2.5 to 3.0 us). A store landed in 2.1 us in the median, in 4.2 to 5.4 behind four loads of query rows, and in 7.6 and 8.0 where FFN_B's weights stood in the queue as well.
- **The start of WO.** In the first layer tile 0 starts at 386.10, 1.0 us behind the last copy (forecast 0.1), and tile 3 at 398.44, 13.4 us behind it; the text said "near 13". That was right, but not the gain of 4.3 us a sequence: the last addition of WO0 starts 31.1 and 31.2 us behind the copy, against 32.4 and 30.9 before. Tile 3 comes behind a stop of 2.3 us, and for 3 us its matmuls take 0.63 us instead of 0.39. In the second layer tile 3's addition was to come 14.4 us behind the copy and came 23.1 us behind (646.2 to 669.27). Timeline of the second layer:

```profile
645.60 0.58 ACT L1456 COPY heads_raw<-bank 128x512 f32<-128x512 f32 x1 [1.91 <-PE bank L1020]
...
649.45 3.35 DVE L1247 RECIPROCAL features<-features 128x512 f32<-128x512 f32 x1 [24.49 <-DMA features<-raw_rows_dram]
...
652.84 1.71 DVE L1257 TENSOR_TENSOR features<-features 128x512 f32<-128x512 f32 x1
...
654.59 1.37 DVE L1259 CAST ops<-features 128x512 fp32r<-128x512 f32 x1
...
656.78 0.77 PE L802 MATMUL bank<-ops 128*128 128x512 f32 x1 [11.23 <-issue]
...
660.33 3.34 DVE L1247 RECIPROCAL features<-features 128x512 f32<-128x512 f32 x1
...
663.70 0.69 DVE L1257 TENSOR_TENSOR features<-features 128x512 f32<-128x512 f32 x1
664.43 0.43 DVE L1259 CAST ops<-features 128x512 fp32r<-128x512 f32 x1
...
669.27 0.69 DVE L1093 TENSOR_TENSOR x<-bank,x 128x512 f32<-128x512 f32 x1 [2.49 <-PE bank L804]
```

  The forecast began its chain at the second half's copy. But the first half's sums came so late (649.45) that its reciprocal, operations and tile 0 stood on VectorE ahead of the second half's, and TensorE was idle 11.2 us and at half clock after it (0.77 us for a matmul of 128x512). Forecast +4 us for both sequences, measured +19.9.
- **The port.** Forecast +3. The same lines show it: beside GpSimd's split of weights and its bias addition the multiply takes 1.71 us and the copy 1.37, without them 0.69 and 0.43. The bias addition is slowed too, to 1.71 us from 1.28. The effect is there, also for the copy, which reads one operand; by these lines it makes the first half's three operations 3.8 us instead of 1.8, but what that costs the whole wasn't tried apart.
- **GpSimd and MOE_A's weights.** GpSimd's operations take 1.27, 0.61 and 1.27 us, and no mask held TensorE for more than 0.7 us in the changed kernel. The step could have gone wrong: two of the experiments moved these operations ahead of masks and paid for it. The weights' move wasn't tried alone; from WO0's last addition to the first scores of the second attention pass 138.3 and 138.4 us, 140.0 and 138.1 before, which leaves no room for a cost.
- **The sum.** Forecast +15.4 us, that is +20 for the first attentions (port apart), -9 from WO0 on, -3 for the second attentions and +4 from WO1 on; measured +55, -2, +9 and +20 between the profiled executions. Taken one at a time, the runs give about 70 us to the reciprocals in the loops (clock included) and 26 us to the shape of the loads; that the two add up isn't shown.

## What to carry to other kernels

When two engines are coupled through a short ring and both are above 90% busy, price added work (or a wait for a DMA placed in the order of the other) at the stop that it makes and at the matmuls behind it at half clock; here the second part was larger than the first, and moving or cutting the work helped little or not at all, only having less of it. Invert a sum before it is broadcast, not after. Put 16 or 32 rows outermost in a DMA, as the loads by head did, and not 2 or 4 heads, and put an operation that waits for a DMA where nothing that TensorE needs stands behind it.

## What the runs showed of the hardware that was not expected

- Two or three stops of TensorE of 1.3 to 2.6 us inside a unit went with 17 to 23 us at half clock (35.6 us at 0.76, 38.9 us at 0.74, 40.1 us at 0.71). Stops of under 1 us in a row did it too (36.6 us at 0.67 in the run with the pieces). In the kernel before a stop of 2.36 us had left the clock at 1.00, and two units (30.7 us at 0.89 with 0.6 us of idle time before the change, 33.3 us at 0.74 with 0.3 us in the one-column run) fell without a stop: a stop makes a fall likely, and is neither needed nor enough.
- Loads of rows at 53 and 109 GB/s with 2 and 4 heads outermost, against 415 GB/s for the store of the same data.
- GpSimd's power: 0.55 us for 128x1, 82 us for 128x512. VectorE's reciprocal: 3.35 us for 128x512, 3.35 us for 64x512, 0.95 us for 128x128, 0.25 us for 128x16.
- A store in the same queue behind four loads of 192 KB landed 4 to 6 us after its issue instead of 2, and 8 us with a load of 1024 KB ahead of it too.
